# Graph attention with its output steps one and two slots later, and attention's output banks opened by the first product

## What is computed

```
def gat_layer(x, adj, W, a_self, a_neigh, b):        # 8 heads of 32 features
    feat = einsum('nf,hfo->hno', x, W)
    e = leaky_relu(attn_self[:, :, None] + attn_neigh[:, None, :], 0.2)
    e = e + MASK_VAL * (1.0 - adj)
    alpha = softmax(e, axis=-1)
    out = einsum('hnm,hmo->hno', alpha, feat) + b[:, None, :]
    return elu(out.transpose(1, 0, 2).reshape(N, -1))

x = x + gat_layer(gat_layer(ctx, layernorm(x), ...), layernorm(x), ...)   # per graph
x = x + mixture of 8 experts, 2 per token (layernorm(x))
x = x + learned adjacency (ctx, layernorm(x))
x = x + o @ Wo, o = causal attention with 32 heads of 128
x = x + mixture of 32 experts, 8 per token, and a shared one
```

## Time and profile before

| | us |
|---|---|
| median of 3 runs | 1138.37 |
| lowest and highest | 1137.56, 1141.92 |
| the profiled execution | 1142.99 |
| its span, first to last instruction | 1141.2 |
| TensorE busy | 1045.9 |
| DVE busy | 847.6 |
| ACT busy | 605.4 |
| POOL busy | 415.2 |

### The profile page before, as it was taken

One profiled execution on the slowest core, in us unless ns is written; L12 is line 12 of the kernel. 1 busy time (PEld: TensorE's weight loads), 2 busy tenths in 40 slices (PEclk: granted clock), 3 DMA queues, 4 the chain that ended last, 5 costly groups with the idle time before them and its releaser, 6 DMA issues.

```text
span 1141.2 us, 20328 instructions
## 1 busy us (share of the span) xinstructions
PE 1045.9 (92%) x6046; PEld 851.3 (75%) x6046; DVE 847.6 (74%) x2613; ACT 605.4 (53%) x1686; POOL 415.2 (36%) x358
## 2 busy tenths in 40 slices
PE   5999988399999458999999999999998999999997
PEld 3556565246666247899999999999987888888886
DVE  6878687427775478977777777777777888888887
ACT  3578585243333238777777777777864222222221
POOL 4688686360000433332333333322322232323321
PEclk9999697569999769999999999999999999999999
DMA  8900000311111221101011010000010111111111
GB/s 251 373 15 1 1 2 1 104 56 45 43 47 47 69 98 38 47 1 38 6 43 38 1 34 1 2 1 2 2 42 15 43 42 55 41 55 41 45 52 37
DMA packets 55459, 53.46 MB, mean 47 GB/s; under 512 B 5536, under 2 KB 48864, under 8 KB 55376
## 3 DMA queue, kind: packets, MB, share of 16 engines
q1 hardware_dynamic: 52560, 46.87, 13.0%
q0 software_dynamic: 1536, 4.20, 1.1%
q10 hardware_dynamic: 1280, 1.38, 0.5%
HBM read 43.25 MB, written 9.18 MB: 46 GB/s over the span
## 4 chain that ended last, share of the span: by engine, by line
PE 75%; POOL 8%; DVE 7%; issue 4%; ACT 4%; DMA 2%; another core or an unknown queue 0%; ACTq 0%; DVEq 0%; POOLq 0%
PE bank L57 13%; PE bank L58 13%; PE bank L59 13%; PE bank L921 7%; PE bank L942 5%; PE bank L818 4%; PE bank L843 4%; PE bank L826 3%; PE bank L931 3%; POOL rest L1362 3%; PE bank L943 2%; POOL alpha L1365 2%; PE bank L616 1%; PE bank L900 1%; POOL g_pos L1340 1%
## 5 line engine op out<-in xcount | busy, mean ns | idle before, releaser
L1435 POOL TENSOR_TENSOR rot_s<-swap,rq 128x512 f32<-128x512 f32 x64 | 88.4, 1382 | 198.5 <-ACT swap L1214 198.5
L1090 ACT ACTIVATE silu<-bank 128x512 f32<-128x512 f32 x66 | 39.5, 599 | 173.5 <-PE bank L59 173.5
L1962 DVE TENSOR_TENSOR o_ring<-bank,o_ring 128x256 fp32r<-128x256 f32 x128 | 54.3, 424 | 83.8 <-ACT o_ring L1243 83.0
L1227 ACT ACTIVATE prob<-prob,pmin 128x128 f32<-128x128 f32 (+1 forms) x256 | 113.2, 446 | 2.8 <-DVE pmin L1943 2.8
L921 PE MATMUL bank<-kv,norm 128*128 128x128 f32 (+1 forms) x512 | 106.5, 331 | 6.2 <-DVE norm L1936 6.1
L1784 DVE SCALAR_TENSOR_TENSOR xs<-bank,wt,xs 128x256 f32<-128x256 f32 x264 | 109.0, 475 | 0.1
L1383 POOL TENSOR_TENSOR gate_r<-gate_w,gate_r 128x256 fp32r<-128x256 f32 x31 | 36.4, 1175 | 177.2 <-ACT gate_r L1083 177.2
L1243 ACT ACTIVATE o_ring<-bank 128x256 fp32r<-128x256 f32 x128 | 48.4, 378 | 80.1 <-PE bank L943 79.9
L57 PE MATMUL bank<-wo_r,o_ring 128*128 128x256 f32 x256 | 84.1, 328 | 0.0
L1943 DVE CUSTOM_DVE_ANT_0 prob<-bank,causal 128x128 f32<-128x128 f32 (+1 forms) x256 | 80.1, 350 | 0.3 <-PE bank L921 0.2
L1955 DVE TENSOR_SCALAR prob<-prob,pinv 128x128 f32<-128x128 f32 (+1 forms) x256 | 75.9, 339 | 4.6
(11 more groups left out here) (287 smaller groups left out, 3119.0 us busy)
## 6 DMA issues: line engine op xcount, KB each, us to landing
gate_w<-in_Wg SPq DMA_DIRECT2D x33, 128.0 KB, 2.1
up_w<-in_Wu SPq DMA_DIRECT2D x33, 128.0 KB, 2.2
down_w<-in_Wd SPq DMA_DIRECT2D x33, 128.0 KB, 2.2
w_all<-in_w_gate SPq DMA_DIRECT2D x8, 512.0 KB, 10.2
w_all<-in_w_up SPq DMA_DIRECT2D x8, 512.0 KB, 10.4
w_all<-in_w_down SPq DMA_DIRECT2D x8, 512.0 KB, 10.5
wq_g<-in_Wq SPq DMA_DIRECT2D x4, 1024.0 KB, 5.6
wo_g<-in_Wo SPq DMA_DIRECT2D x4, 1024.0 KB, 5.5
```

Of the source, the lines that this page charges most:

```text
L1227: ins = act.activation(prob[:, u % 4, nt * P:nt * P + (nt + 1) * P], prob[:, u % 4, nt * P:nt * P + (nt + 1) * P], ACT.Exp, bias=pmin[:, u ...
L1435: pool.tensor_tensor(rot_s[:, m % 2].rearrange("p (b n) -> p b n", b=2), swap[:, m % 2].rearrange("p (b n) -> p b n", b=2), bcast(tab[:, 1 ...
```

## The change

In graph attention `divide` stands one slot later (11 + 4j), `exp_out` and `positive` two (12 + 4j) and `elu` two (13 + 4j); `turn_x1`, `add_x1`, `measure` and `inverse` follow by two slots each, and so do the loop's end and, for the third graph, the slots of its normalisation, transposition and routing. In attention the sixteen matmuls of noughts, their operand, its memset and its semaphore go, and the first product of a unit with `r == 0` carries the start flag, once for the whole bank.

```
-        nought = sb("nought", [P, 2 * D], BF16)
...
-        LAST = ALL + 11
-        NORM_AT, TURN_AT, ROUTE_AT = (ALL, ALL + 2, ALL + 8), (ALL + 2, ALL + 4, ALL + 9), (ALL + 4, ALL + 6, ALL + 10)
+        LAST = ALL + 13
+        NORM_AT, TURN_AT, ROUTE_AT = (ALL, ALL + 2, ALL + 10), (ALL + 2, ALL + 4, ALL + 11), (ALL + 4, ALL + 6, ALL + 12)
...
-                    if (r := round_at(k, 17)) is not None:
+                    if (r := round_at(k, 19)) is not None:
                         turn_x1(r)
...
-                    if r == 0:
-                        pe.wait_ge(S["nought_set"], 1)
-                        pe.matmul(W_BANK[b2][:], nought[:, 0:P], nought[:], start=True, stop=False)
                     for nt in range(NT):
                         mm = split_product(
...
-                            [wo_r[:, g % 2, j, r, :] for j in range(2)], False, r == REP - 1 and nt == NT - 1)
+                            [wo_r[:, g % 2, j, r, :] for j in range(2)], r == 0 and nt == 0, r == REP - 1 and nt == NT - 1)
...
-                    if (j := quad_at(k, 1)) is not None:
+                    if (j := quad_at(k, 3)) is not None:
                         exp_out(j)
...
-                if (j := quad_at(k, 1)) is not None:
+                if (j := quad_at(k, 3)) is not None:
                     positive(j)
...
-                if (r := round_at(k, 20)) is not None:
+                if (r := round_at(k, 22)) is not None:
                     inverse(r)
...
-                    if (j := quad_at(k, 1)) is not None:
+                    if (j := quad_at(k, 2)) is not None:
                         divide(j)
-                    if (j := quad_at(k, 2)) is not None:
+                    if (j := quad_at(k, 4)) is not None:
                         elu(j)
-                    if (r := round_at(k, 18)) is not None:
+                    if (r := round_at(k, 20)) is not None:
                         add_x1(r)
-                    if (r := round_at(k, 19)) is not None:
+                    if (r := round_at(k, 21)) is not None:
                         measure(r)
...
-                dve.memset(nought[:], 0.0).then_inc(S["nought_set"], 1)
```

More of the change, by code:

```diff
@@ L320, in build @@
             "s_ready", "s_shift", "p_exp", "p_inv", "p_norm", "pT_ready", "pT_copied",
-            "o_ready", "o_high", "o_copied", "o_used", "wo_added", "nought_set",
+            "o_ready", "o_high", "o_copied", "o_used", "wo_added",
             "out_done")}
```

## The result

The changed kernel takes **1131.6 us** (median) against 1139.8 for the kernel before on the same chip: ratio **0.9936**, 95% interval 0.9914 to 0.9957, or 7.3 us less (4.9 to 9.8). The forecast was 14.1 less, 1124.3. The direction is right, the time lies within the range of 1116 to 1135, and about half of the forecast gain is missing.

A forecast was written before the change was run, and what follows sets the result against it. TensorE was taken to bound the kernel nearly everywhere, except a graph attention stretch with a ring of four engines and a falling clock. Terms -3.3 - 6.9 - 0.5 + 0.3 - 3.4 - 0.3 = -14.1 us gave 1124.3 us, range 1116 to 1135.

The forecast's parts named there:

- Waits for `g_out`: Graph attention: POOL's and ACT's waits for the division's result should fall from 26.3 and 32.3 us to under 8 each.
- The ring: Graph attention, 69.14 to 184.86 us: heads passed round four engines; later slots leave POOL as limit, -3.3 us, bounds 0 and -3.3.
- The floor: Graph attention: POOL's five instructions and the gap to the next, 8.70 us a quad, taken as what is late next.
- The clock: Graph attention, 69.14 to 184.86 us: half of the low clock's 13.7 us cost goes, -6.9 us, between 0 and -13.7.
- Other signs I had named: Graph attention: mean clock over 0.85, and 100 to 109 us from the third `g_pos` to the fourteenth.
- The rival at 1117.5: Graph attention: the clock stays up, only idle time bringing it down; stretch 98.7 us, whole 1117.5 us; chance 0.17.
- Waits handed on: Graph attention gives nothing, POOL and ACT waiting for next scores or minima instead; noughts alone remain, 1134.7 us; chance 0.12.
- `features(7)`: TensorE's slot 53 needs the bank that the later `add_x1(4)` frees: a new wait, +0.3 us, from nothing to 2.25.
- The first part: Graph attention until 69.14 us: TensorE is busy throughout, so removing waits gives nothing there, 0.
- The tail: After 184.86 us, last quads running down: same chain with other work between, -0.5 us, between -1.5 and +1.
- Noughts: Attention: sixteen opening matmuls go at 0.21 us each, -3.4 us; their memset on DVE before attention goes, -0.3 us.

The follow-up runs named there:

- e14: The changed kernel, unchanged, executed once more for a second profile; span 1132.5 us.
- e3: The changed kernel with the division alone back in its old slot, exponential, positive part and sum still late; 1129.8 us, 0.9915 of the kernel before.
- e2: The kernel before with all slots of graph attention moved as in the change, noughts kept; 1133.4 us, ratio 0.9943.
- e9: The kernel before, unchanged, executed once more for a second profile; span 1140.3 us.
- e5: The kernel before with four further matmuls of noughts in each of the sixteen openings in attention; 1152.5 us, ratio 1.0108.
- e1: The kernel before with only the sixteen matmuls of noughts and their memset taken out, graph attention as before; 1135.3 us, ratio 0.9972.
- e7: The changed kernel with DVE's copy of `alphaT` ahead of `edges` and `leak` in its slot; 1127.0 us, 0.9877 of the kernel before.
- e6: The changed kernel with TensorE's `edges` of the next head ahead of the transposition in each slot; 1126.2 us, 0.9890 of the kernel before.
- e8: The changed kernel with one further matmul of constants ahead of each head's `edges` matmul in graph attention; 1128.5 us, 0.9919 of the kernel before.
- e10: The changed kernel with the division in its old slot and DVE's copy of `alphaT` ahead of `edges`; 1123.4 us, 0.9887 of the kernel before.
- e11: The changed kernel with division in its old slot, DVE's `alphaT` copy ahead of `edges`, TensorE's `edges` ahead of its transposition; 1121.6 us, 0.9863 of the kernel before.
- e12: The changed kernel with division and exponential back in their old slots, only positive part and what follows late; 1133.9 us, 0.9956 of the kernel before.
- e16: The changed kernel with POOL's sum for odd heads replaced by a one-operand product and minimum on 328 columns; 1125.0 us, 0.9887 of the kernel before.

## Why the prediction was right, and where it was wrong

- **Waits for `g_out`**: right. Under 8 us each was forecast, 3.0 and 2.0 measured; DVE's wait for the quad's matmuls (L636) fell from 20.6 to 0.3.
- **The ring, -3.3 us: the step that failed.** "What is late next is POOL itself": it was not. POOL waits 26.8 us for ACT's copy, and its quads of five instructions at full clock have a mean of 9.04 us against 9.06 before, where 8.70 was forecast; that they stay at 9.0 I had named as a sign of being wrong. Eleven of them and the 3.0 us of other work are 102.4, so the ring gave nothing in the first profile. In e14 such quads have a mean of 8.64, but there the long ones fell into the lower clock. The floor was wrong too, 8.34 and not 8.70, but nothing hung on it. I had costed the exponential's and positive part's new places, and let the division pass with "behind the `edges` of one more head": the rule to name what is queued behind a moved instruction was not kept for `divide`, behind which stand an even head's `edges` and the copy that TensorE waits for. With the division left alone (e3) such quads have a mean of 8.66. That the division's place is the cause rests on these profiles; the runs of e3 overlap those of the changed kernel.
- **The clock, -6.9 us: the direction right, the size a guess.** I had taken half of the low time of 44 us for want of a reason. The low time in the middle stretch fell from 41.2 to 28.9 us, and to 18.8 in e14. At the price of the forecast, 13.7 / 44 = 0.31 us for each us low, 28.9 us cost 9.0; with the ring at 102.4 that is 111.4, against 110.8 measured. By this estimate the clock gave 13.7 - 9.0 = 4.7 of the 6.9 us, and the greater part of what is missing is the ring's 3.3. e14 does not fit the same price: 18.8 us low would cost 5.8 and leave 104.5 for the ring. Over the executions of one kernel the span grows by 0.29 us (e2, 12 executions) and 0.25 (changed kernel, 13) for each us at the lower clock, as its mean granted clock gives it, but by anything from 0.01 to 0.33 in the five sets of the kernel before. So the failure of the ring's term is seen in the quads, while the exact split of the measured -4.9 (-5.1 from e9 to e14) between ring and clock stays open.
- **Other signs I had named**: the mean clock in the stretch was over 0.85 as forecast (0.87 and 0.91); from the third to the fourteenth `g_pos` it took 110.5 and 111.1 us, above the 100 to 109.
- **The rule of the Trainium skill** ("TensorE: Matmul & The Clock Gate", Part 1), by which the clock would stay up: the changed kernel is crowded closer and its clock does stay up longer, but 28.9 us of the stretch are still low. The rival at 1117.5 did not come; its 98.7 us needs the ring at POOL's floor, which the quads of 9.04 us do not reach.
- **Waits handed on**: my third rival is what happened in part. I gave it the whole of the gain or nothing and no place; the place is the waits that took over: ACT's for TensorE's scores (13.0 to 32.9 us), POOL's for ACT's copy and DVE's for POOL (11.7 each to 26.8 and 21.7).
- **`features(7)`**: +0.3 forecast, from 0 to 2.25; measured 1.35 us once (1.0 in e14), over the 1 us that I had allowed, and the clock fell during that wait, at 147.3:

```profile
147.99 2.05 PE L588 MATMUL bank<-w,actT 128*128 128x256 f32 x4 [1.35 <-DVE xs L1584]
```

- **The first part, 0**: 5.6 us shorter in the first profile, 0.6 to 1.8 in e14. TensorE being busy for all of it was no reason for nothing, since it was busy at half clock.
- **The tail, -0.5**: -0.1 and +1.1; the one within the bounds of -1.5 and +1, the other just past them.
- **Noughts, -3.4 and -0.3**: the price of one is right, 0.19 to 0.22 us by e5; the sum is mis-sized in the trace, 1.7 us, since TensorE then waits for DVE at the start of attention. The runs of e1 say 3.2 us with an interval that holds both.

## What to carry to other kernels

Moving a late step further back takes away the wait that the profile names, but what counts is what then stands behind the moved step on its own engine: list it for each engine apart, and move only the steps whose engine really waits (here, by the profiles, ACT's exponential and not DVE's division). A ring of four engines, none full, is limited by its order; its length must be read from quads at full clock that hold the same work, and a floor of one engine's busy time is a bound, not a forecast. Put the copy or the matmul that another engine waits for ahead of work that nobody waits for yet: e7 came out 0.9877 against 0.9936 by that, nearly as much again as the whole change.

## What the runs showed of the hardware

- DVE's step on `alpha` and the mask, two operands, takes 0.42 us beside no work of POOL, up to 1.55 us where it meets POOL's sum of two operands (8 of 14 meetings in the changed kernel last over 1.0), and up to 0.87 where it meets only `rest`. Ten profiles (before, after, e14, e3, e6, e7, e8, e10, e11, e12) have 85 halves above 1.0 us, of 1.08 to 1.55. All of them overlap such a sum and none overlaps only `rest`, which has one operand. With an instruction of one operand as long in place of the sum (e16) there is none above 0.85. The Trainium skill ("SBUF — State Buffer", "Who interferes with whom") has DVE and GpSimd share a port for which the one waits while the other holds it; these rows agree: a step of 0.42 us alone takes over 1.0 beside the sum. Beside an instruction of one operand it waits as well, but less, up to 0.45 us though `rest` lasts 1.9 to 2.0.
- On POOL a product with a sum on 128x320 took 0.46 us, a product with a minimum on 128x328 1.31 us.
- A TensorE that is busy without a gap may run at the lower clock: 20.40 of 20.40 us in the kernel before. In e8, with more matmuls, 13.8 us of the stretch are still low.
- Two executions of the changed kernel differ by 3.8 us before head 18, one with the clock's first rise at 41.5 us and the other with it at 66.4.
